# A fused AdaLN block (linear attention and mixture of experts): start reordered, a table product on GpSimd, one output bias for two batches, another order of the down tiles

## What is computed

```python
mod = (silu(c) @ wmod).reshape(2, 6, 1, -1)           # sa, ca, ga, sb, cb, gb per batch
h = layernorm(x) * (1 + ca) + sa
Xn = layernorm(h, gamma, beta)
Q, K, V = split(Xn @ W_in + b_in)
K, V = rotary(K), rotary(V)                           # cos and sin of position times frequency
A = 0.5 * sum_over_tokens(K/|K| * V/|V|) + 0.5        # one row per batch
x = x + ga * ((A * Q) @ W_out + b_out + h)
h = layernorm(x) * (1 + cb) + sb
x = x + gb * (routed(h) + shared(h))                  # 8 experts, top 2, H = 352; shared H = 704
```

## Time and profile before

| | us |
|---|---|
| median of 3 runs | 702.92 |
| lowest and highest | 700.83, 703.11 |
| the profiled execution's own time | 700.52 |
| its span, first to last instruction | 698.7 |
| TensorE busy | 669.8 |
| VectorE busy | 504.1 |
| ScalarE busy | 276.4 |
| GpSimd busy | 174.9 |

### The profile page before, as it was taken

One profiled execution on the slowest core, in us unless ns is written; L12 is line 12 of the kernel. 1 busy time (PEld: TensorE's weight loads), 2 busy tenths in 40 slices (PEclk: granted clock), 3 DMA queues, 4 the chain that ended last, 5 costly groups with the idle time before them and its releaser, 6 DMA issues.

```text
span 698.7 us, 10766 instructions
## 1 busy us (share of the span) xinstructions
PE 669.8 (96%) x3760; PEld 554.1 (79%) x3760; DVE 504.1 (72%) x1097; ACT 276.4 (40%) x535; POOL 174.9 (25%) x221
## 2 busy tenths in 40 slices
PE   7699999999998999999999999999999999999993
PEld 3477677778877888788787887899898989989892
DVE  4887789737898886556767654596876969678662
ACT  3554354535343333412013014264553736456340
POOL 1233133210012110000000022035464444642404
PEclk9999999999999999999999999999999999999998
DMA  8912221013244633321230343466586755755415
GB/s 332 388 31 95 59 64 46 31 31 136 62 155 148 216 106 111 109 87 42 76 129 0 99 152 103 133 200 111 170 172 128 200 89 199 115 169 93 52 17 68
DMA packets 41872, 82.53 MB, mean 118 GB/s; under 512 B 5163, under 2 KB 13373, under 8 KB 41286
## 3 DMA queue, kind: packets, MB, share of 16 engines
q1 hardware_dynamic: 33382, 62.06, 26.7%
q0 software_dynamic: 8448, 19.93, 15.4%
HBM read 59.93 MB, written 23.22 MB: 119 GB/s over the span
## 4 chain that ended last, share of the span: by engine, by line
PE 59%; DVE 10%; issue 2%; DMA 2%; ACT 1%; POOLq 0%; SPq 0%; POOL 0%; DVEq 0%; ACTq 0%
PE bank L1667 16%; PE bank L1669 16%; PE bank L1668 16%; PE bank L1962 4%; PE bank L1940 2%; DMA sdraw<-in_L_ffn_sw_down 1%; PE bank L1967 1%; PE bank L1920 1%; DMA ewst<-in_L_ffn_w_up 1%; DVE m L1221 1%; DVE rows L1257 1%; DVE st L1059 1%; DVE u L1247 1%; DVE mw L1226 1%; DVE hx L1269 1%
## 5 line engine op out<-in xcount | busy, mean ns | idle before, releaser
L647 POOL DMA_INDIRECT out_rows<-y,si x40 | 61.9, 1548 | 95.0 <-DVE y L1597 87.7
L1667 PE MATMUL bank<-ht,ew 128*128 128x288 f32 x256 | 76.8, 300 | 0.0
L1668 PE MATMUL bank<-ht,ew 128*128 128x288 f32 x256 | 75.6, 295 | 0.0
L1669 PE MATMUL bank<-ht,ew 128*128 128x288 f32 x256 | 75.6, 295 | 0.0
L1667 PE MATMUL bank<-xt,sgu 128*128 128x512 f32 x176 | 69.5, 395 | 3.2 <-DVE xt L1276 2.0
L1669 PE MATMUL bank<-xt,sgu 128*128 128x512 f32 x176 | 68.7, 390 | 0.0
L1668 PE MATMUL bank<-xt,sgu 128*128 128x512 f32 x176 | 68.7, 390 | 0.0
L1667 PE MATMUL bank<-wkv,xt 128*128 128x512 f32 x128 | 53.9, 421 | 2.2 <-DVE xt L1088 2.2
L636 POOL DMA_INDIRECT picked<-h_d,gi x40 | 47.1, 1178 | 24.1 <-issue 9.8
L1668 PE MATMUL bank<-wkv,xt 128*128 128x512 f32 x128 | 50.5, 395 | 0.0
L1669 PE MATMUL bank<-wkv,xt 128*128 128x512 f32 x128 | 50.5, 394 | 0.0
(11 more groups left out here) (343 smaller groups left out, 1692.2 us busy)
## 6 DMA issues: line engine op xcount, KB each, us to landing
xring<-in_L_attn_X SPq DMA_DIRECT2D x32, 256.0 KB, 2.8
ewst<-in_L_ffn_w_gate SPq DMA_DIRECT2D x8, 704.0 KB, 5.3
ewst<-in_L_ffn_w_up SPq DMA_DIRECT2D x8, 704.0 KB, 5.4
slots<-in_L_wmod SPq DMA_DIRECT2D x4, 1024.0 KB, 7.0
x_d<-rows SPq DMA_DIRECT2D x16, 256.0 KB, 2.0
h_d<-hx SPq DMA_DIRECT2D x16, 256.0 KB, 2.0
xrow<-x_d SPq DMA_DIRECT2D x16, 256.0 KB, 2.7
out_rows<-xrow SPq DMA_DIRECT2D x16, 256.0 KB, 2.1
```

The source lines that it names most:

```text
L647: pool.indirect_dma_start(out=out, out_offset=bass.IndirectOffsetOnAxis(ap=si[0:CR[j], par, j:j + 1], axis=0), in_=y[0:CR[j], j, :], in_of ...
L1667: nc.tensor.matmul(dst, a[0], b[0], start=first, stop=False)
L1668: nc.tensor.matmul(dst, a[0], b[1], start=False, stop=False)
L1669: return nc.tensor.matmul(dst, a[1], b[0], start=False, stop=last)
```

## The change

1. On VectorE the copy of `mrow` moves ahead of `x_statistics(0)`, and `x_statistics(1)` behind `weights_lo(0)`. GpSimd's `first_power(1)` moves behind `second_power(0)`.
2. The multiplication of the two tables moves from VectorE, where it stood behind `x_statistics(2)`, to GpSimd, between `first_power(1)` and `second_power(1)`. ScalarE's square of sine moves ahead of `normed(1)`, and `bias_row_hi(1)` behind it.
3. The token pieces of the second tile (`tokens_hi(1)`, `tokens_lo(1)`) move from the loop to its front: on ScalarE ahead of the first `k_row`, on VectorE ahead of `x_statistics(2)` and `modulated(2)`.
4. The bias rows of both batches come from one matmul chain: VectorE spreads `qah` over 128 columns, 32 for each of high and low part by batch, into the place of `bk` (which the K/V stage has used up). Four blocks by two parts of W_out are 8 products, whose rows 0 to 63 hold the high and 64 to 127 the low part of both batches. `y_bias` adds the halves and handles 32 rows per batch, in six instructions. ScalarE's `shared_in_hi(2)` waits for these products, not for the last `misc`.
5. `J_OF` becomes (0, 1, 4, 2, 3): the half tile is at the third place of five, not at the fourth.

```diff
-J_OF = (0, 1, 2, 4, 3)
+J_OF = (0, 1, 4, 2, 3)
...
+        qas = bk[:, :].rearrange("p (k s b r) -> p k s b r", k=DC, s=2, b=B)
...
             first_power(0)
-            first_power(1)
...
             second_power(0)
+            first_power(1)
+            pool.wait_ge(table_in, 32)
+            pool.tensor_tensor(cos, cos, sin, ALU.mult).then_inc(sincos, 1)
             second_power(1)
...
             weights_hi(1, (1, 2, 3))
-            bias_row_hi(1)
-            normed(1)
             act.wait_ge(sincos, 1)
             nc.scalar.activation(sin, sin, ACT.Square).then_inc(sinsq, 1)
+            normed(1)
+            bias_row_hi(1)
+            tokens_hi(1)
...
-            act.wait_ge(misc_mm, len(MISC))
+            act.wait_ge(h_mm, 1)
             shared_in_hi(2)
...
+                    if b:
+                        dve.wait_ge(a_ready, B)
+                        for i in range(2):
+                            src = qah[:, :, i, :].rearrange("p b k -> p k b").unsqueeze(3).to_broadcast([P, DC, B, Q4])
+                            last = dve.tensor_copy(qas[:, :, i, :, :], src)
+                        last.then_inc(a_ready, 1)
...
-            x_statistics(0)
             dve.wait_ge(first_mm, 2)
             dve.tensor_copy(mrow[:, 1, :], bank[W_BANK][:, :]).then_inc(first_row, 1)
+            x_statistics(0)
...
+                link(dve.tensor_tensor(junk[:, :], bank[H_BANK][:, :], bout[:, :], ALU.add))
+                link(dve.tensor_tensor(junk[0:half, :], junk[0:half, :], bank[H_BANK][half:P, :], ALU.add))
+                for b in range(B):
+                    at = slice(b * Q4, (b + 1) * Q4)
+                    link(dve.tensor_tensor(junk[at, :], junk[at, :], bc_s[at, b, :], ALU.add))
+                    link(dve.tensor_tensor(junk[at, :], junk[at, :], bc_ga[at, b, :], ALU.mult))
...
-            def h_matmul(b):
-                pe.wait_ge(a_ready, b + 1)
+            def h_matmul():
+                pe.wait_ge(a_ready, B + 1)
                 for k in range(DC):
-                    last = product3(bank[H_BANKS[b]][:, :], [qah[:, b, s, k:k + 1].to_broadcast([P, P]) for s in range(2)],
-                                    [wo[:, s, k, :] for s in range(2)], k == 0, k == DC - 1)
+                    columns = bk[:, k * P:(k + 1) * P]
+                    nc.tensor.matmul(bank[H_BANK][:, :], columns, wo[:, 0, k, :], start=k == 0, stop=False)
+                    last = nc.tensor.matmul(bank[H_BANK][:, :], columns, wo[:, 1, k, :], start=False, stop=k == DC - 1)
```

More of the change, by code:

```diff
@@ L262, in build @@
         T_BANKS, K_BANKS, V_BANKS, W_BANK, MISC_BANK = (0, 1), (2, 4), (3, 5), 6, 7
-        M_BANKS, H_BANKS = ((0, 1, 2, 3), (4, 5, 0, 1)), (7, 6)
+        M_BANKS, H_BANK = ((0, 1, 2, 3), (4, 5, 0, 1)), 7
         Y_BANKS, T2_BANKS, LG_BANK, PART_BANK = (2, 3), (6, 7), 1, 0
@@ L793, in _ @@
                 k_row(t)
-                if t + 1 < NT:
+                if 1 <= t < NT - 1:
                     tokens_hi(t + 1)
@@ L1181, in _ @@
             dve.wait_ge(gb_ready, 1)
-            x_statistics(1)
             dve.wait_ge(spread_mm, 3)
@@ L1186, in _ @@
             weights_lo(0)
+            x_statistics(1)
             tokens_lo(0)
@@ L1191, in _ @@
             bias_rows(1)
+            tokens_lo(1)
             x_statistics(2)
-            dve.wait_ge(table_in, 32)
-            dve.tensor_tensor(cos, cos, sin, ALU.mult).then_inc(sincos, 1)
             for t in range(NT):
@@ L1227, in m_block_lo, with y_bias @@
                     .then_inc(m_lo, 1)
-            def y_bias(b):
-                at = slice(0, P) if b == 0 else slice(Q4, 2 * Q4)
-                row = junk[at, :]
-                dve.wait_ge(h_mm, b + 1)
-                link(dve.tensor_tensor(row, bank[H_BANKS[b]][at, :], bout[at, :], ALU.add))
-                link(dve.tensor_tensor(row, row, bc_s[at, b, :], ALU.add))
-                link(dve.tensor_tensor(row, row, bc_ga[at, b, :], ALU.mult))
+            def y_bias():
+                half = B * Q4
+                dve.wait_ge(h_mm, 1)
+                link(dve.tensor_tensor(junk[:, :], bank[H_BANK][:, :], bout[:, :], ALU.add))
[4 more added lines that the diff above has]
+                    link(dve.tensor_tensor(junk[at, :], junk[at, :], bc_ga[at, b, :], ALU.mult))
             def y_bias_rows():
@@ L1302, in _ @@
             dve.wait_ge(bout_in, 16)
-            y_bias(0)
-            y_bias(1)
+            y_bias()
             for b in range(B):
@@ L1859, in _ @@
             pe.wait_ge(misc_read, len(MISC))
-            h_matmul(0)
-            h_matmul(1)
+            h_matmul()
             m_matmul(1)
```

## The result

| | us | ratio to the kernel before |
|---|---|---|
| before, median of 8 runs | 703.01 (700.83 to 705.78) | |
| after, median of 8 runs | 707.44 (704.59 to 712.35) | 1.0057, interval 1.003 to 1.0085 |
| after, the profiled execution | 708.12, span 706.4 | |

The change makes the kernel slower, by 4.0 us of 703 going by the ratio. The forecast was 2.2 us slower, with 706.9 as its upper end. The two profiled executions lie 7.6 us apart, so some of what they differ by is not the change's.

The account below looks back on a forecast made before the run. Bounds: a VectorE, ScalarE and GpSimd chain at the start, VectorE at the bias, TensorE in the experts. 0.0 + 0.0 + 2.2 took the profiled 700.52 to 702.7, median 705.2; own range 704.0 to 706.2, with rivals 701.0 to 706.9.

Parts of the forecast that it names:

- Edits 1 and 2: Start: earlier `mrow` copy and moved pieces, table product on GpSimd; gains and delays sum to 0.0 us.
- The neighbour's hold: Start, second tile: GpSimd's 2.3 us table product holds VectorE's two-tile instructions, delaying `modulated(1)` by 1.8 us.
- Edit 3: Output bias in 8 products, not 24: TensorE saves 3.7 us, but VectorE sets the pace, so 0.0 us.
- Edit 4: Experts, half tile third of five: 0.36 us more in each of seven, 0.3 less at the end, +2.2 us.
- the hold that never comes (1): Start: GpSimd's long product does not hold VectorE, everything up to the experts 1.75 us earlier; 703.4 us, chance 17%.
- the one that comes again and again (2): Start: VectorE's two-tile instructions hold GpSimd's product repeatedly, `s1` 1.6 us late; 706.8 us, chance 10%.
- (3): Experts: the half tile's new place does not stall TensorE, only the end's 0.3 us remains; 702.6 us, chance 13%.
- X + 3.87: Experts: forecast start of the fifth place, X being the third's start; TensorE stands 0.26 us for it.
- (4): Output bias: the removed products count after all, -3.7 + 2.2; 701.4 us, chance 7%.
- the 47% stated: Whole kernel: chance given for a time measured as no change, between 700.8 and 705.0 us.

Follow-up runs that it names:

- the doubled product: Changed kernel with the table product done twice on GpSimd, first into an unused tile; one execution, no ratio given, second tile's transposes 1.9 us later.

## Why the prediction missed

**Edits 1 and 2 (forecast 0.0)** held: -0.2 in the trace up to the bias, 0.9993 in time. The neighbour's hold was the right mechanism: 1.6 us on one instruction as forecast, shown by the doubled product; against the product on VectorE it costs 1.0 us in the K/V stage.

**Edit 3 (forecast 0.0)** is the step that failed. That TensorE's 3.7 us would bring nothing was right, as was the reason: VectorE, whose row products stood 0.2 us from where they had been. But I costed the removed matmuls by their time alone. They are also instructions, and 16 of them fewer move TensorE's later instruction loads, one of them by about 6 us and onto a store on which the shared experts wait 160 us later. That is 0.9 to 1.9 us in five profiles, and 2.0 and 1.2 us in the two measurements of the edit alone, where the forecast had 0.0. No row of mine spoke of it; the trace of before has the loads, and the DMA queue's line in the page names them.

**Edit 4 (forecast +2.2)** held: 0.38 us in each of seven experts against 0.36, and 0.25 at the end against 0.3; 2.4 us in all.

The sum of the parts, -0.2 + 1.6 (the mean of 2.0 and 1.2) + 2.4, is 3.8 us, and 4.0 were measured. Of the rivals, the hold that never comes (1) and the one that comes again and again (2) are both out, (3) fell with the five-place row at X + 3.87, and (4) by VectorE's row products. The range had an upper end for costs of known kinds only. Two slips of reckoning changed little: 702.92 + 2.2 is 705.1 and not 705.2, and the chances given for no change come to more than the 47% stated (18 + 17 + 13 is 48 without rival 4).

The extra 3.6 us between the two profiled executions lie for the most part in two terms: the fall of the clock (1.64), which comes and goes in one program, and ScalarE's wait ahead of the first expert (1.49). The latter is open: a wait of 2.4 to 3.2 us there stands in 7 of the 13 profiles of kernels with the new start and in none of the 7 with the old one, where it is 1.3 or less. So the new start may bring it about; its measured ratio, 0.9993, would then hold a gain and this loss together. No run told these apart.

## What to carry to other kernels

Read a difference of two single executions step by step before crediting it to the edit: a second profile of the unchanged kernel showed 1.6 us that the first did not. When instructions go or come in number, look at what the instruction loads behind them now fall on, above all on a transfer that someone waits for; a few small instructions of padding tell in one profile whether that is it. Count instructions as the trace does, since one call can be two. And where GpSimd and VectorE both read two tiles, try the long operation on the engine on which it is shorter: here that was worth 1.0 us.

## What the hardware showed that I had not expected

- A 16 KB instruction load occupies one DMA engine for about 1.4 us (2.2% of 16 engines in 4 us; 0.9 to 1.6 us in the loads near 340 us of the 20 profiles), and a 256 KB store beside it landed after 3.5 to 4.2 us in five of five profiles, after 2.0 in fourteen of fourteen without such a load.
- TensorE's instruction loads follow its instruction count: 258 instructions from one to the next in the median, and a load 5.5 to 6.4 us later with 16 matmuls fewer, 11.0 us later with 32 fewer.
- A held instruction is shown as a long one, not as an idle one: VectorE's 0.75 us row instruction reads 2.35 and 2.76 us, and no wait is printed.
- The granted clock fell to half for some 3 us behind waits of TensorE in one of two executions of the same program, and in 9 of 20 profiles at 216 us, where it cost 1.5 to 1.7 us; at 20 to 32 us it came in 11 of 20, all but once at no lasting cost.
- A product of fp32 operands, 128 columns, shows as two matmuls and took 0.23 us (16 in 3.74 us), as much as one of fp32r with 512 columns.
